# A fused window attention and mixture-of-experts kernel: projections in 64-row tiles in the score banks, gates in two banks

## The reference

```python
x = x + conv(_ln_c(x))           # _ln_c: over the 64 channels
t = to_tokens(x)
x = from_tokens(t + ffn(_ln_t(t)))

# conv: windows of 8 x 8 on x.reshape(B, H//8, 8, W//8, 8, C), 4 heads of 16
q = xw @ Wq + bq ; k, v = split(xw @ Wkv + bkv)
attn = softmax(q * 16**-0.5 @ k.T + rel_bias)
out = (attn @ v) @ Wproj + bproj

# ffn: 8 experts of 64 x 64, the top 2 per token
p, i = top_k(softmax(t @ router_w + router_b), 2) ; p = p / sum(p)
out = sum(p * (t @ expert_w[i] + expert_b[i]))
```

## Time and profile before

| | |
|---|---|
| median of 3 runs | 1537.11 us (1533.65 to 1537.75) |
| profiled execution: time, span | 1533.56 us, 1531.7 us |
| mean granted clock of PE | 0.984 |
| PE busy | 1333.5 us (87%) |
| DVE busy | 1195.6 us (78%) |
| POOL busy | 886.8 us (58%) |
| ACT busy | 884.2 us (58%) |
| DMA | 90.23 MB, mean 59 GB/s |

### The profile page before, as it was taken

One profiled execution on the slowest core, in us unless ns is written; L12 is line 12 of the kernel. 1 busy time (PEld: TensorE's weight loads), 2 busy tenths in 40 slices (PEclk: granted clock), 3 DMA queues, 4 the chain that ended last, 5 costly groups with the idle time before them and its releaser, 6 DMA issues.

```text
span 1531.7 us, 49805 instructions
## 1 busy us (share of the span) xinstructions
PE 1333.5 (87%) x18247; PEld 824.9 (54%) x18432; DVE 1195.6 (78%) x2486; ACT 884.2 (58%) x1672; POOL 886.8 (58%) x731
## 2 busy tenths in 40 slices
PE   4488999988898999988898899998989999999976
PEld 3255555555555555555555555555555555555541
DVE  7548888977776888987787688898778777787764
ACT  5356666646555666655555566664655566565631
POOL 0246555668654655658856455566875656656532
PEclk9999999999999999999999999999999999999998
DMA  6012333222122233222122233322212222122221
GB/s 169 1 31 57 73 77 76 60 51 55 41 50 53 71 77 77 57 70 53 39 58 50 57 81 77 72 64 51 59 38 54 53 58 55 38 56 50 58 58 35
DMA packets 95212, 90.23 MB, mean 59 GB/s; under 512 B 26653, under 2 KB 62045, under 8 KB 95070
## 3 DMA queue, kind: packets, MB, share of 16 engines
q1 hardware_dynamic: 95070, 88.30, 24.5%
HBM read 35.83 MB, written 17.83 MB: 35 GB/s over the span
## 4 chain that ended last, share of the span: by engine, by line
DVE 33%; PE 25%; POOL 16%; issue 16%; ACT 3%; DMA 3%; DVEq 1%; SPq 1%; POOLq 1%; another core or an unknown queue 1%; ACTq 0%
PE bank_g L502 7%; DVE t_g L954 5%; PE bank_p L375 5%; PE bank_y L513 5%; POOL ln L1050 4%; DVE mx L849 3%; DVE x L871 3%; DVE sums L798 3%; DVE sums L790 3%; POOL prob L1038 2%; DVE prob L842 2%; POOL rstd L1022 2%; PE bank_e L473 2%; POOL t_g L1060 2%; DVE bank_e L883 2%
## 5 line engine op out<-in xcount | busy, mean ns | idle before, releaser
L954 DVE TENSOR_TENSOR t_g<-t_t,bank_g 128x512 f32<-128x512 f32 x384 | 262.9, 685 | 164.3 <-PE bank_g L502 153.7
L513 PE MATMUL bank_y<-t_g,w_exp 128*64 128x512 f32 x1024 | 272.5, 611 | 30.4 <-issue 15.6
L653 ACT ACTIVATE prob<-prob 128x512 f32<-128x512 f32 x256 | 159.9, 626 | 202.7 <-POOL prob L1038 202.6
L1038 POOL TENSOR_TENSOR prob<-prob,mx 128x512 f32<-128x512 f32 x256 | 262.0, 1046 | 2.5 <-DVE mx L849 2.5
L1060 POOL TENSOR_TENSOR t_g<-t_t,g_copy 128x512 f32<-128x512 f32 x128 | 164.8, 1288 | 169.5 <-ACT g_copy L685 166.5
L375 PE MATMUL bank_p<-xn,w_qkv 128*64 128x256 f32 x1536 | 215.2, 400 | 33.2 <-POOL xn L1032 17.7
L1029 POOL TENSOR_TENSOR xn<-xt,rstd 128x512 f32 (+1 forms) x64 | 81.7, 1277 | 240.4 <-PE bank_p L375 238.3
L842 DVE TENSOR_TENSOR prob<-bank_s,rel 128x1024 f32<-128x1024 f32 x128 | 156.4, 1222 | 72.1 <-PE bank_s L401 64.5
L657 ACT ACTIVATE prob_t<-bank_t 128x512 f32<-128x512 f32 x256 | 152.3, 595 | 66.2 <-PE bank_t L416 66.2
L1050 POOL TENSOR_TENSOR ln<-ln,mhalf 128x8 f32<-128x8 f32 x64 | 104.8, 1637 | 145.8 <-DVE ln L885 145.8
L502 PE MATMUL bank_g<-g_t,gate_sel 128*128 128x512 bf16 x390 | 151.7, 389 | 42.9 <-DVE t_g L954 41.3
(11 more groups left out here) (108 smaller groups left out, 2359.4 us busy)
## 6 DMA issues: line engine op xcount, KB each, us to landing
t_t<-t_rout SPq DMA_DIRECT2D x256, 128.0 KB, 3.7
x_in<-in_x SPq DMA_DIRECT2D x68, 256.0 KB, 3.2
r_b<-recip_rows SPq DMA_DIRECT2D x64, 256.0 KB
out_y<-y_out SPq DMA_DIRECT2D x128, 128.0 KB, 2.3
r_in<-sum_b SPq DMA_DIRECT2D x64, 16.0 KB
recip_rows<-r_out SPq DMA_DIRECT2D x64, 16.0 KB, 1.4
rel<-in_relb SPq DMA_DIRECT2D x1, 256.0 KB
gate_sel<-in_sel SPq DMA_DIRECT2D x1, 256.0 KB
```

The source lines that it names most:

```text
L513: mm(B_Y[C * a:C * a + C, :], w_exp[:, pair, :], t_g[:, (2 * pair + a) % TG, :], start=False, stop=(pair == MIXES // 2 - 1), skip_group_ch ...
L653: A(prob[:, i], prob[:, i], ACT.Exp).then_inc(p_ready.sem, 1)
L954: V.tensor_tensor(t_g[:, u % TG, :], t_t[:, p, u % 2, :], B_G[:, :], ALU.mult).then_inc(tg_dve.sem, 1)
L1038: G.tensor_tensor(sc, sc, mx[:, i, :].unsqueeze(2).broadcast_to([P, 2 * HEADS, NTOK]), ALU.subtract).then_inc(s_shifted.sem, 1)
```

## The change

It has four parts.

- The three projections use tiles of 64 rows by 64 columns: 24 matmuls of 128 columns each in place of 12 of 256. The two row halves write the two banks of `bank_s`. Keys and values are one run of 16, queries a second run of 8. `w_qkv` loses its zero half. The copies on ACT read from `bank_s`; `copy_q` is one instruction.
- `bank_p` is free of projections, and gates alternate between `bank_g` (even u) and `bank_p` (odd u); gate u waits for the reader of gate u - 2. The sums of the probabilities stay in `bank_p`.
- Every engine's slot is in a new order. On ACT, the exponentials `exps(j, 1)` stand at the end of the slot before. On DVE routing is cut at 0-4, 5-8, 9-19 in place of 0-8, 9-13, 14-19. On POOL, both deviations stand behind gate 2.
- `statistics` is cut in two (`total_sums`, `variances`) and moves from the end of the eighth take slot into the first power slot.

```diff
+            def project(g, parts):
+                if parts == QUERIES:
+                    pe.wait_ge(k_ready.sem, k_ready.at(g, 2))
+                    pe.wait_ge(v_ready.sem, v_ready.at(g, 1))
+                else:
+                    pe.wait_ge(xn_ready.sem, xn_ready.at(g, 2))
+                    if not (isinstance(g, int) and g == 0):
+                        pe.wait_ge(s_biased.sem, s_biased.at(g))
...
+                for i in parts:
+                    for n in range(2):
+                        for ab in range(2):
+                            for half in range(2):
+                                rows = slice(C * half, C * half + C)
+                                src = xn[rows, :, :].rearrange("p c (hh n ab i l) -> p n ab i (c hh) l", hh=2, n=2, ab=2, l=4)
+                                dst = B_S[C * ab:C * ab + C, half, 256 * (i == 2):256 * (i == 2) + 256]
...
+                                last = mm(dst[:, n], w_qkv[rows, i, :], src[:, n, ab], start=True, stop=True,
+                                          skip_group_check=True)
                 last.then_inc(qkv_done.sem, 1)
...
             def prob_sums(g):
-                if isinstance(g, int) and g == LAST:
+                if not (isinstance(g, int) and g == 0):
                     pe.wait_ge(sum_copied.sem, sum_copied.at(g))
-                else:
-                    pe.wait_ge(v_ready.sem, v_ready.at(g + 1, 1))
+                if not (isinstance(g, int) and g < 2):
+                    pe.wait_ge(tg_dve.sem, tg_dve.at(g - 2))
...
             def gates(g, u):
-                if u and u - 1 in ON_POOL:
-                    pe.wait_ge(g_copied.sem, g_copied.at(g, ON_POOL.index(u - 1) + 1))
+                if u == 1:
+                    pe.wait_ge(sum_copied.sem, sum_copied.at(min(g + 2, LAST) if isinstance(g, int) else g + 2, 1))
+                elif u and u - 2 in ON_POOL:
+                    pe.wait_ge(g_copied.sem, g_copied.at(g, ON_POOL.index(u - 2) + 1))
                 elif u:
-                    pe.wait_ge(tg_dve.sem, tg_dve.at(g, ON_DVE.index(u - 1) + 1))
-                mm(B_G[:, :], gate_sel16[:, u, :], g_t[:, :], start=True, stop=True).then_inc(gate_done.sem, 1)
+                    pe.wait_ge(tg_dve.sem, tg_dve.at(g, ON_DVE.index(u - 2) + 1))
+                mm(B_GATE[u % 2][:, :], gate_sel16[:, u, :], g_t[:, :], start=True, stop=True).then_inc(gate_done.sem, 1)
...
             def copy_k(g, p, e):
                 act.wait_ge(qkv_done.sem, qkv_done.at(g, 1))
-                A(k_m[:, p, :, e, :].rearrange("p v (a l) -> p v a l", l=4), turned(B_P[:, :]), ACT.Identity,
+                A(k_m[:, p, :, e, :].rearrange("p v (g s) -> p g v s", g=2),
+                  B_S[:, :, 0:256].rearrange("p g (v s) -> p g v s", v=PAIRS), ACT.Identity,
                   bias=k_bias[:, e:e + 1], scale=k_mask[:, e:e + 1]).then_inc(k_ready.sem, 1)
...
                 if work.power is not None:
                     inverse_deviation(work.batch, work.power)
-                if mixing:
-                    gate(j - 3, 1 - p, 2)
-                if work.power is not None:
                     inverse_deviation(work.batch, work.power + 1)
```

More of the change, by code:

```diff
@@ L533, in slot @@
                     gates(j - 3, 0)
-                if routing_on:
-                    turn_tokens(j - 2)
+                    gates(j - 3, 1)
                 if work.take:
@@ L539, in slot @@
                     turn_probs(j, 1, work)
-                if mixing:
-                    gates(j - 3, 1)
                 if routing_on:
-                    logits(j - 2)
-                if attending and work.take:
-                    turn_probs(j, 1, work)
+                    turn_tokens(j - 2)
                 if mixing:
@@ L548, in slot @@
                 if projecting:
-                    project(j + 1, 0)
+                    project(j + 1, QUERIES)
+                if attending and work.take:
+                    turn_probs(j, 1, work)
+                if routing_on:
+                    logits(j - 2)
                 if mixing:
+                    gates(j - 3, 3)
                     experts(j - 3, 0)
-                    gates(j - 3, 3)
                 if attending:
@@ L612, in first_take @@
                 for m in range(2):
[L613 removed]
+                    take(batch, t, r, m, (B_T[:, :], B_S[:, 0, :])[m])
                 for m in range(2):
@@ L706, in slot @@
                     copy_k(j + 1, 1 - p, 1)
+                    copy_v(j + 1)
+                if work.take:
+                    take(work.batch, *work.take, 0, B_T[:, :])
+                if attending and not work.take:
+                    copy_probs(j, 1)
                 if routing_on:
                     copy_tokens(j - 2)
-                if work.take:
-                    take(work.batch, *work.take, 0, B_T[:, :])
+                if projecting:
+                    copy_q(j + 1, 1 - p)
+                if attending and work.take:
+                    copy_probs(j, 1)
                 if attending:
-                    copy_probs(j, 1)
                     exps(j, 2)
@@ L716, in slot @@
                 if attending:
+                    copy_probs(j, 2)
                     exps(j, 3)
[L718 to L723 removed]
                 if routing_on:
@@ L965, in slot @@
                     sum_planes(work.batch, *work.sums)
+                if work.up:
+                    total_sums(work.batch)
                 if mixing:
@@ L1069, in slot @@
                     shift(j, 3)
-                if work.power is not None:
-                    inverse_deviation(work.batch, work.power)
                 if mixing:
@@ L1074, in slot @@
                 if work.power is not None:
+                    inverse_deviation(work.batch, work.power)
                     inverse_deviation(work.batch, work.power + 1)
```

123 lines of the change are left out of this document (51 added, 72 removed).

## The result

| | before | changed |
|---|---|---|
| median | 1537.01 us (1533.65 to 1537.75, 4 runs) | 1515.49 us (1511.7 to 1523.94, 4 runs) |
| ratio | | 0.987, 95% interval 0.982 to 0.992 |
| profiled execution, span | 1533.56, 1531.7 us | 1511.88, 1510.0 us |
| mean granted clock of PE | 0.984 | 0.973 |

The change is faster, by 1.3%. The forecast was 1471 us, and 1515 lies outside its range of 1436 to 1510. A third of the gain came.

The account below looks back on a forecast made before the run. PE, DVE and POOL lay within 2 or 3 us of being the bound; afterwards a PE-DVE ring limits idle slots. Gains 29 + 27.6 + 3.6 + 4 + 10.9 - 12.6 = 62.5 us off 1533.56 give 1471, range 1436 to 1510.

Parts of the forecast that it names:

- Projections 1.3 us less on PE a slot: PE: 24 matmuls on 64-row tiles, four at once, take 1.55 us where twelve took 2.86; gain 1.3 us a slot.
- rival of pairs: PE: 64-row tiles run only two at a time, so the 24 matmuls take 2.8 us; whole 1504 us, chance 0.16.
- Ring of 19.9 us: Idle slots: K/V run, logits, DVE and next K/V run form a closed chain of 19.9 us, 21.1 before.
- PE's leg: PE's part of that closed chain, from the K/V run to DVE's first routing step: 5.9 us.
- DVE's leg: DVE's part of that chain, first routing step through next slot's bias: 12.6 us to the bias, 13.85 with bias and signal.
- Power slots 12.6 us lost: POOL's nine power slots: gate first exposes the wait for the copied gate, 1.4 us each, 12.6 us lost.
- A change of tiling 0.10 us: PE: 17 tiling changes a slot, 13 before, cost 0.4 us more; rival with drains of 0.35 each: 1484 us, chance 0.06.
- Statistics 10.9 us: DVE: three batches' statistics, 3.6 us each, are hidden in the first power slot where POOL is the bound; gain 10.9 us.
- Take slots 21.3: The 24 take slots with sums fall to 21.3 us, 1.15 us less each; gain 27.6 us.
- Second gate bank worth only what DVE's leg needs: Gates' second bank pays only by letting DVE run its part of the chain without stops: 1.14 us.
- own signs of being wrong: The forecast is wrong if idle slots stay above 20.7 us or power slots get longer than 24.
- no gain: New waits (K/V behind bias, POOL behind copied gate) eat PE's saving; whole within 5 us of 1533, chance 0.05.

Follow-up runs that it names:

- both moves: Changed kernel with DVE's reciprocals ahead of gate 0 and POOL's gate 2 again between the two deviations: 1464.7 us, 0.955 of the kernel before.
- the run over 128 rows: Changed kernel with each of the 24 projection matmuls over all 128 rows, half of the weights zero: 1561.3 us, 1.019 of the kernel before.
- reciprocals first: On DVE, reciprocals moved ahead of gate 0: in the changed kernel 1488.1 us; as a control in the kernel before 1531.5 us against 1535.2.
- POOL's old order: Changed kernel with POOL's power slots again as first deviation, gate 2, second deviation: 1496.1 us, 0.975 of the kernel before.

## Why the prediction was wrong

Where the time went in the profiled executions, by intervals of one slot (from one token mean to the next on DVE, so that what stands late in a slot counts in that interval), sums in us:

| stretch | before | changed | both moves |
|---|---|---|---|
| start, first interval, three take slots without sums | 194.6 | 180.2 | 180.8 |
| 21 intervals of take slots | 471.6 | 455.3 | 447.2 |
| 15 intervals, from the eighth take slot on, 3 x 5 | 346.7 | 368.1 | 341.3 |
| 9 other idle intervals of the first batches | 189.8 | 188.3 | 181.4 |
| 12 idle intervals of the last batch | 252.3 | 249.5 | 239.7 |
| end | 76.7 | 68.6 | 72.5 |
| span | 1531.7 | 1510.0 | 1462.8 |

The third line holds the statistics and the power slots. There the changed kernel loses 21 us, and both moves bring 27 back; in the 21 idle intervals it gains 4 us, where both moves gain 21. The first and the last line of the changed kernel gain 22.5 us together, where the forecast had 7.6 for the start and nothing for the end: without this unpriced part the change would have gained about 7 us, not 21.7.

- *Projections 1.3 us less on PE a slot*: right, and with it the rival of pairs falls. 1.66 us measured for 1.55, and the run over 128 rows gave back 46 us where 45 to 55 were expected.
- *Ring of 19.9 us*: its shape was right (K/V run, logits, DVE, bias), and PE's leg, 6.2 for 5.9. The step that failed is DVE's leg, "the same instructions as today in another order, 13.76 less the waits". That took the instructions as the length, and forgot that `normalise` has a wait of its own, which the old order covered: in the earlier trace rows no wait for r_b is to be seen, since `normalise` came 8 us after its reciprocal. In the new order the bias of pair 0 and gate 5 (1.14 and 0.60 us in the earlier trace rows) no longer stand before it, some of the waits in between are gone, and it comes up 6 us after (gate 4 ends at 1269.18). The DMA path of 7.1 us is then the longest, 1.12 us a slot, 57 us in all, of which reciprocals first took 40 away, for 27 us of device time. "The queue's order is untouched" and that the sums are copied one step earlier on ACT was all that the forecast said of DMA; the queue was, the distance was not.
- *Power slots 12.6 us lost*: the direction right, the size wrong. The forecast priced the wait for the copied gate alone (1.4 us). It did not follow POOL's list on to gate 6, for which PE waits, nor ask what PE's standstill does to the clock: 5.18 us of waiting and then about 5 us at half speed. Undoing POOL's order alone gave 19 us back. No run separates the wait from the clock in these 19.
- *A change of tiling 0.10 us*: nothing speaks for a drain of up to 0.38. The leg of 6.2 us holds the wait of 0.47 for t_n, and the run of 16 is followed by another tiling after 1.03 us. By how much a change differs from 0.10 was not measured.
- *Statistics 10.9 us*: right as far as measured, 10.7 by putting them back.
- *Take slots 21.3*: 21.7 measured, and 21.3 with both moves.
- *Second gate bank worth only what DVE's leg needs*: right as to its place, and its price when taken away (95 us) larger than any figure I had.

Of the forecast's own signs of being wrong both came true: idle slots stayed at 20.8 to 21.0 (limit 20.7), and slots with deviations took over 24 us (26.4 and 27.5).

With both faults mended the kernel takes 1464.7 us, 6 us from the forecast of 1471. That this is so near is in part luck. POOL's old order takes back the 12.6 us that the forecast had as lost, so its sum for this kernel is 75 us of gain, near 1458. By the table, in the profiled executions, 68.9 us came: 24.4 in the 21 take intervals for a forecast 24.2, 21.0 in the 21 idle ones for 25.2, 5.4 in the third line for about 18, and 18.0 at the start and the end for 7.6. The take slots (21.3) and the idle slots of the last batch (20.0 for 19.9) bear the forecast's terms out; the third line fell short by about as much as the start and the end brought unpriced.

One sum of the prediction is wrong in itself: the rival "pairs only", by its own terms (5 + 27.6 + 3.6 + 4 + 10.9 - 12.6 = 38.5 us), comes to 1495 and not 1504. The rival "no gain" named waits that eat the saving (power 24.5, idle 20.9); it had nearly the right idle slot, for a reason that it did not name, and little weight at 0.05; its time, within 5 us of 1533, did not come.

## What to carry to other kernels

When an order is changed, measure for each instruction that waits for a DMA how long before it the request was made, and lay the new order against the DMA's own time: a wait that is not in the old trace can be covered, not absent. When something long is moved on a side engine, follow that engine's list to the next instruction that the matmul engine needs. A stall like the 5.18 us here is paid twice, by the wait and by the half clock after it.

## What the runs showed of the hardware

Four tiles of 64 x 64 with 128 float32 columns run at 1.03 us for 16 matmuls, the same as 16 matmuls in 32 x 64 tiles. Over 128 rows, two tiles at a time, the same 24 matmuls took 205.5 us in the whole kernel instead of 116.7.

Half clock comes behind waits of PE, but no single figure of the waits gives the mean clock. With POOL's new order PE waits for POOL up to 6.7 us in one piece in the changed kernel, and 6.8 with reciprocals first (11 waits each, 44.3 and 53.9 us in all), and all 22 runs of kernels that have that order and two gate banks show a mean granted clock of 0.964 to 0.974. With POOL's old order (that move alone, and both moves) the longest such wait is 3.9 us (17 waits, 34.4 and 34.1 us), and the clock is 0.974 to 0.981, above 0.975 in seven of eight runs. The longest wait and the sum fall together here, so these runs do not tell which counts. The run with one gate bank speaks against the longest alone: its longest wait for POOL is 4.4 us (9 waits, 31.4 us) and none at a gate is over 2.2, and its clock is the lowest, 0.952. In the kernel before, a wait of 0.89 us for DVE at 307.18 is followed by half speed too (granted clock 0.50 from 307.50 to 310.00, a projection run of 1.98 us where it takes 1.08).

In the kernel before with reciprocals first, the same kernel ran between 1523.0 us at 0.989 and 1538.9 us at 0.972: 1.7% of clock, 1% of time, the spread of one kernel from run to run.
